# A relational graph network on one core: where TensorE and VectorE wait in the 2352 edge tiles

## What is computed

```python
msgs = h[src] * norm[:, None]
out = jax.ops.segment_sum(msgs, dst, num_segments=N)
...
inv_deg = 1.0 / jnp.maximum(cnt[dst, edge_type], 1.0)
...
def _rgcn_layer(X, W, root, bias, gamma, beta, src, dst, etype, inv_deg):
    h = jnp.einsum('ni,rio->rno', X, W)
    msg = h[etype, src] * inv_deg[:, None]
    agg = jax.ops.segment_sum(msg, dst, num_segments=X.shape[0])
    out = agg + X @ root + bias
    mu = jnp.mean(out, axis=-1, keepdims=True)
    var = jnp.mean(jnp.square(out - mu), axis=-1, keepdims=True)
    out = (out - mu) * jax.lax.rsqrt(var + EPS) * gamma + beta
    out = jax.nn.elu(out)
    return out + X
```

## Time and profile before

| | us |
|---|---|
| median of 3 runs | 5235.64 |
| lowest and highest run | 5233.83, 5237.05 |
| span of the profiled execution | 5905.4 |
| TensorE busy in it | 4806.4 (81%) |
| VectorE busy | 3711.0 (63%) |
| GpSimd busy | 3267.9 (55%) |
| ScalarE busy | 1418.0 (24%) |

### The profile page before, as it was taken

How to read it: one execution, slowest core, us unless ns; L and a number is a source line. 1 busy time by engine, 2 the same in 40 slices (tenths; PEclk the granted TensorE clock), 3 DMA queues, 4 the chain that set the end, 5 groups by cost and what they waited for, 6 DMA issues and landing times.

```text
span 5905.4 us, 80081 instructions
## 1 busy us (share of the span) xinstructions
PE 4806.4 (81%) x20415; PEld 3355.2 (57%) x20415; DVE 3711.0 (63%) x9969; ACT 1418.0 (24%) x3629; POOL 3267.9 (55%) x3256
## 2 busy tenths in 40 slices
PE   5878876777888887888887888887888888777776
PEld 4544432345666665666664666665666665556555
DVE  7998885565666664555554555555556555566665
ACT  1046653213555551111111111111111111011011
POOL 0058871003666664666664666665666664666664
PEclk8999998999999998999998999998999998888888
DMA  1000016312555555555555555555555555444444
GB/s 49 1 1 1 1 21 228 143 61 89 159 156 161 162 158 170 161 157 155 159 157 150 162 156 159 159 155 161 155 158 155 159 159 152 144 143 145 143 140 126
DMA packets 398886, 772.61 MB, mean 131 GB/s; under 512 B 77327, under 2 KB 166113, under 8 KB 398424
## 3 DMA queue, kind: packets, MB, share of 16 engines
q0 software_dynamic: 150720, 386.19, 24.2%
q1 hardware_dynamic: 246824, 380.53, 19.2%
q10 hardware_dynamic: 1008, 1.84, 0.1%
HBM read 652.04 MB, written 115.89 MB: 130 GB/s over the span
## 4 chain that ended last, share of the span: by engine, by line
PE 65%; issue 13%; DVE 12%; another core or an unknown queue 5%; ACT 2%; DVEq 2%; DMA 1%; ACTq 0%; SPq 0%
PE psum L736 24%; PE psum L758 23%; PE psum L690 5%; PE psum L807 3%; DVE arena L1429 3%; PE psum L840 2%; PE psum L793 2%; DVE arena L1571 2%; DVE arena L1303 2%; DVE arena L1290 2%; PE psum L700 1%; DVE arena L1238 1%; PE psum L622 1%; DVE emat L1409 1%
## 5 line engine op out<-in xcount | busy, mean ns | idle before, releaser
L584 POOL DMA_INDIRECT msg<-h_table,g_rel x1880 | 1795.6, 955 | 1088.5 <-issue 419.9
L1429 DVE TENSOR_TENSOR arena<-arena,psum 128x256 f32 x2940 | 1224.7, 417 | 1434.8 <-PE psum L758 970.4
L758 PE MATMUL psum<-msg,emat 128*128 128x256 f32 x4704 | 1519.7, 413 | 547.7 <-issue 323.1
L758 PEld LDWEIGHTS psum<-msg,emat 128*128 128x128 f32 x4704 | 892.9, 202 | 1021.7 <-issue 795.6
L1409 DVE TENSOR_SCALAR emat<-iota,node,weight 128x128 f32<-128x128 f32 x2352 | 862.9, 368 | 139.4 <-issue 58.8
L736 PE MATMUL psum<-arena,emat 128*128 128x256 f32 x3200 | 908.1, 405 | 6.3 <-issue 6.1
L584 POOL DMA_INDIRECT msg<-h_table,g_src x472 | 457.0, 968 | 726.3 <-PE psum L758 591.0
L736 PEld LDWEIGHTS psum<-arena,emat 128*128 128x128 f32 x3200 | 647.5, 204 | 134.0 <-issue 35.5
L566 POOL DMA_INDIRECT placed_rows<-leaving,idx x300 | 439.6, 1465 | 423.3 <-issue 416.7
L584 POOL DMA_INDIRECT hout<-h_table,g_rel x472 | 451.3, 956 | 275.4 <-issue 110.2
L793 PE MATMUL psum<-arena,emat 125*128 125x453 f16 x2000 | 448.0, 358 | 85.9 <-DVE arena L1303 85.9
(11 more groups left out here) (253 smaller groups left out, 5331.1 us busy)
## 6 DMA issues: line engine op xcount, KB each, us to landing
emat<-count_blocks SPq DMA_DIRECT2D x496, 256.0 KB
more_blocks<-count_blocks SPq DMA_DIRECT2D x372, 256.0 KB
count_blocks<-emat SPq DMA_DIRECT2D x200, 256.0 KB
h_table<-hout SPq DMA_DIRECT2D x100, 512.0 KB
msg<-h_table,g_rel POOLq DMA_INDIRECT x1880
arena<-h_table SPq DMA_DIRECT2D x24, 512.0 KB
msg<-h_table,g_src POOLq DMA_INDIRECT x472
hout<-h_table,g_rel POOLq DMA_INDIRECT x472
```

The lines of the kernel that those rows point to most:

```text
L584: pool.indirect_dma_start(out=slots[n % RING], out_offset=None, in_=table[:, :], in_offset=bass.IndirectOffsetOnAxis(ap=rows[:, t:t + 1], ...
L758: pe.matmul(agg_ps[n % NPS][:, 0:D], emat[:, n % BODY, :], slots[n % RING], start=True, stop=True).then_inc(s_mm, 1)
L1429: dve.tensor_tensor(a, a, agg_ps[n % NPS][:, 0:D], ALU.add).then_inc(s_acc, 1)
```

## The change

TensorE keeps its three waits in pass 0 alone. In the relational passes it waits for the edge matrix only. VectorE waits for the bank of tile n - 4 and for the landed rows of tile n before it makes the matrix of tile n, and it makes the matrix three tiles ahead (`LEAD`) instead of eight. The wait for VectorE's own last addition is the same number as the new wait for the bank (with `LEAD` = 3 and four banks), and stays for the last three tiles of a pass, which make no matrix.

```diff
@@ -47,6 +47,7 @@
     HALF = 8
+    LEAD = 3
@@ -752,9 +753,9 @@
                     pe.wait_ge(s_em, n + 1)
-                    pe.wait_ge(s_msg[n % RING], (n // RING + 1) * 16)
-
-                    pe.wait_ge(s_acc, ACC0 + n + 1 - NPS)
+                    if q == 0:
+                        pe.wait_ge(s_msg[n % RING], (n // RING + 1) * 16)
+                        pe.wait_ge(s_acc, ACC0 + n + 1 - NPS)
                     pe.matmul(agg_ps[n % NPS][:, 0:D], emat[:, n % BODY, :], slots[n % RING],
                               start=True, stop=True).then_inc(s_mm, 1)
@@ -1406,6 +1407,8 @@
             def edge_matrix(q, t):
 
                 n = q * NT + t
+                dve.wait_ge(s_acc, ACC0 + n + 1 - NPS)
+                dve.wait_ge(s_msg[n % RING], (n // RING + 1) * 16)
                 dve.tensor_scalar(emat[:, n % BODY, :], iota[:, 0:P], node[:, t:t + 1],
@@ -1418,12 +1421,14 @@
                     w = wins[t % WINS]
-                    dve.wait_ge(s_acc, ACC0 + n)
                     if q == 0:
+                        dve.wait_ge(s_acc, ACC0 + n)
                         if t not in early:
                             edge_weights(t, w)
-                    elif t + HALF < NT:
-                        edge_matrix(q, t + HALF)
+                    elif t + LEAD < NT:
+                        edge_matrix(q, t + LEAD)
+                    else:
+                        dve.wait_ge(s_acc, ACC0 + n)
                     dve.wait_ge(s_mm, MM0 + n + 1)
@@ -1595,7 +1600,7 @@
                 if q > 0:
-                    for t in range(HALF):
+                    for t in range(LEAD):
                         edge_matrix(q, t)
                     dve.wait_ge(s_ev, q * NW + ONE0)
```

## The result

The changed kernel takes 5246.19 us (median of 15 runs, 5239.28 to 5254.5); the kernel before, run beside it, takes 5236.99 (15 runs, 5233.67 to 5243.99). The ratio is 1.0019 with a 95% interval of 1.0012 to 1.0025: 9.2 us more, a small loss but a real one. It lies inside the 0.2% that I had called "the same"; 15 runs of each tell a smaller difference than that from none. The forecast was 5243.

The account below looks back on a forecast made before the run. GpSimd's gathers, 735 us a pass, were taken as the bound in timed runs. Terms 0 + 0 + 0 + 4.8 + 2 = 7 us on 5235.64 gave 5243 us, 0.13% more, range 5200 to 5290.

Parts of the forecast that it names:

- The bound: Relational passes: GpSimd's gathers, 588 x 1.25 = 735 us a pass, outlast TensorE's 678 us and bound timed runs.
- the term of 0 for the matrix three tiles ahead: Shorter matrix lead delays TensorE 0.35 us a window, 35 us if its chain decides; 0 taken, as gathers decide.
- TensorE's chain decides: Rival: TensorE bounds the relational passes, so the shorter lead costs 35 us and the ends 7: 5278 us; chance 0.28.
- The pass of 760 us: First gather to next pass's first gather: 735 us of gathers, some 5 for last rows landing, 20 between passes.
- Two waits leave TensorE: Dropping two TensorE waits on each of 2352 tiles saves 0; far bound 72 us.
- TensorE's handling of the waits: Rival: a single wait makes some 305 TensorE restarts 0.12 us shorter, saving 37 us: 5199 us; faster case's chance 0.20.
- VectorE's extra wait a tile: One more VectorE wait a tile costs 0, covered by the 0.45 us before the matrix; 118 to 282 us if uncovered.
- Rows waited for at the end of a pass: At a pass's end, matrix and additions queue behind the last rows: 2.0 instead of 0.8 us, 4.8 over four passes.
- VectorE late for its other work: Rival: additions stand three gathers further back, 3.75 us at each pass's end, 15 in all: 5251 us; chance 0.07.
- Start of a pass: First matrix waits for the first rows, 0.35 to 0.5 us later; worst case 2 us over four passes, taken.
- The sum: Lighter TensorE waits 0, VectorE's wait 0, shorter lead 0, pass ends 4.8, starts 2: 7 us added to 5235.64.
- What the profile was to show: Span up by more than the median, up to 40 us; gathers at 1.25 us; one starting matrix; clock steady or lower.

Follow-up runs that it names:

- e1: Kernel before with only the edge matrix made three tiles ahead instead of eight, all waits as before: 5236.07 us, ratio 0.9996 to the kernel before.
- e3: Changed kernel with TensorE keeping its waits for rows and bank in all passes, beside VectorE's: 5247.17 us, ratio 1.0020 to the kernel before.
- e6: Changed kernel, but TensorE instead of VectorE waits for rows in the last 16 tiles of each relational pass: 5238.23 us, ratio 1.0005 to the kernel before.
- e2: Changed kernel with the wait for landed rows back on TensorE, VectorE waiting for the bank only: 5235.13 us, ratio 0.9994 to the kernel before.
- e5: Kernel before (matrix eight tiles ahead) with the relational passes' wait for landed rows moved to VectorE: 5263.81 us, ratio 1.0052 to the kernel before.
- e7: Changed kernel, but TensorE instead of VectorE waits for rows in the first 16 tiles of each relational pass: 5245.55 us, ratio 1.0021 to the kernel before.
- e0: Kernel before, unedited, run again for a second profile (span 5234.2 us): 5235.89 us, ratio 0.9999 to the kernel before.
- e11: Changed kernel with unused places gathering different rows, plus each pass's last window's dense additions one tile earlier: 5210.09 us, ratio 0.9948 to the kernel before.
- e4: Kernel before with one small unused GpSimd memset ahead of each gather in passes 1 and 2: 5238.70 us, ratio 1.0001 to the kernel before.
- e10: Kernel before with two small unused GpSimd memsets ahead of each gather in pass 1: 5238.57 us, ratio 1.0002 to the kernel before.

## Why the prediction was right, and where it was not

**The bound.** The gathers, 1.25 us each, hold in an execution as long as the timed ones: 736 to 738 us from first to last in every relational pass, where I had 735. TensorE's chain was the bound only in the long execution of the earlier trace rows; putting its late releases down to that execution was right. What rests on it was right too: the term of 0 for the matrix three tiles ahead (e1, 0.9996), and against the rival "TensorE's chain decides", 5278, which e1 rules out.

**The pass of 760 us** came out as 767 to 769. The gathers and the stretch between passes were right (19 us against 20), but the last rows with their additions took 10 to 13 us and not 5: I had taken a landing near the start of a pass as typical, and the last tiles' rows land late.

**Two waits leave TensorE: 0.** Right (e3 against the changed kernel, 1.0020 and 1.0019). The rival "TensorE's handling of the waits", 5199, is ruled out with it: the idle time that ended in "issue" in the earlier trace rows was 80.8 us in a pass of the long execution, and is 15.8 in the first relational pass of the second profile.

**VectorE's extra wait a tile: 0.** Right for 572 tiles in a pass (e6). The 0.05 us that I gave as the lower price of a wait stands in no row, and nothing rests on it.

**Rows waited for at the end of a pass: 1.2 us, 4.8 in all.** The mechanism was right (e2 and e6 take the loss away, e5 enlarges it), the size was not: the tails grew by 8.5 us in four passes, 2.1 each. My term was a difference, 2.0 us after against 0.8 before from the last landing to the last addition's start. In the first relational pass it is 3.6 (2907.0 to 2910.59) against 1.5 (2908.5 to 2909.98), and both of my numbers were too small.

- Before: I took 0.67 us for the last product. It takes 1.19 us (two in 2.37 us, at 2907.39), as TensorE's granted clock is 0.50 there, its 1.2 GHz level, after its waits for rows. That makes the term smaller by 0.7.
- After: I let only the matrix and four additions stand behind the last rows. From the last matrix's start, 2908.61, to the last addition's start there are indeed 2.0 us. But that matrix starts 1.6 us after its rows have landed, as VectorE is still at its queue. It was held before tile 585's matrix, and the four dense additions of the last window, 2.4 us that before ran ahead of the landings, now come between that and the last two matrices.

1.2 - 0.7 + 1.6 = 2.1. In the other profiles the picture is the same wherever the trace has the last landing: with the rows waited for by VectorE, three tiles ahead (the changed kernel, e3, e7), the last addition ends 3.6 to 4.4 us after it, and with TensorE waiting (e0, e1, e2, e6) 1.9 to 2.4.

My line through the earlier trace rows could not show this, since there the ring was full and the additions stood in a row anyway. The rival "VectorE late for its other work" had the right engine, 15 us as a price, and the wrong reason, lateness by three gathers. The truth lies between it and my term. That it is the dense additions that make VectorE late is read from the order in the timeline, and e11 bears it out only in part.

**Start of a pass: 2 us.** It cost nothing that can be seen: the first product comes 5.0 to 5.2 us after the first gather, 0.2 us later than before, and the first to last gather is no longer for it (e7). As the term itself said, later tiles catch up. The start in the changed kernel:

```profile
2159.41 0.94 POOL L585 DMA_INDIRECT msg<-h_table,g_rel  x1 [27.66 <-DMA h_table<-hout]
...
2164.13 0.35 DVE L1412 TENSOR_SCALAR emat<-iota,node,weight 128x128 f32<-128x128 f32 x1 [19.08 <-DMA msg<-h_table,g_rel]
...
2164.62 1.19 PE L759 MATMUL psum<-msg,emat 128*128 128x256 f32 x2 [7.44 <-DVE emat L1412]
```

**The sum.** 0 + 0 + 0 + 4.8 + 2 = 7 us, measured 9.2 on the medians. That it came so close is partly luck: one term was too small by 3.7 us and the other too large by 2, and inside the first one two errors of opposite sign partly cancel.

**What the profile was to show.** The 1.25 us stayed, and one matrix stands before the first product. But I said the profiled span would grow by more than the median, up to 40 us, with the ring full: it didn't, because I took what one profile showed for what every profile would show. The clock I took from that profile too. In the first relational pass and the last, the changed kernel has (length; busy time and count of PE, PEld, DVE, ACT, POOL; granted clock, DMA share, GB/s):

```profile
2165.00:2909.00 744.00, 708.25 (x2944) 550.06 (x2943) 507.71 (x1464) 132.82 (x213) 554.45 (x584) 0.98 0.65 192
...
4478.00:5221.00 743.00, 638.62 (x2573) 512.95 (x2574) 537.63 (x1583) 85.72 (x120) 555.92 (x584) 0.90 0.57 168
```

against 0.94 and 0.87 in the earlier trace rows for the second and the last pass. In the second profile of the kernel before they are 0.98 and 0.93. So beside that profile the clock stayed in the first relational pass and fell a little in the last one, as I had said it would.

## What to carry to other kernels

A wait may be moved in the middle of a stream to an engine with time to spare at no price, but at the end of a stage everything that is queued on that engine behind the last item goes onto the path: write down that queue, all of it, before giving the move a price. Compare the span of a profile with the timed runs first; where they differ by 13%, as here, its waits belong to that execution, and a second profile settles more than an argument from the first. And where a gather has unused places, look at which rows they name.

## What was not expected of the hardware

- **Gathers that name one and the same row are slow.** At the end of a pass, where unused places all name row 0, rows land after 7.8 us (median), in mid-pass after 3.2, and at the end of a pass with the unused places spread over the table after 3.1. In one stretch there (2890 to 2895) the DMA engines are busy to 1.00 while they move 143 GB/s, against 0.62 and 186 in mid-pass. It costs 38.8 us of 5240.56, some 0.7%, four times what the change under study is worth, and both kernels have it.
- **GpSimd has 0.3 us free between two gathers, and using half of it is free.** A 0.13 us memset, or two in 0.15, between gathers left the distance of 1.25 us as it was (e4, e10).
- **One execution of a kernel can be 13% longer than the others** (5905.4 against 5234.2 us), with late completions all through it and the same 80081 instructions in it. What made it so long stays open.
- **TensorE's granted clock is a little lower where VectorE waits for the rows, at no cost that the times show.** Its mean over the whole execution was 0.958 to 0.963 in the ten runs of the kernel before, and 0.952 to 0.954 in the eleven of e6, whose times are the same (ratio 1.0005). The full clock is 2.4 GHz and 0.50 of it is the 1.2 GHz level; in the stretch 2904 to 2911, the end of the first relational pass, both kernels have 0.50, after waits for rows. In the changed kernel the last additions waited for VectorE's own queue there, not for TensorE. In the kernel before, the last product stands on the path at that clock, 1.19 us instead of 0.67.
